# Gated delta net: a new order of steps over the engines' queues, and the decayed state made by four VectorE operations per chunk

## The chip, the cores and the metric

The kernel runs on one core of a Trainium2 chip. The metric is the time of one execution on the device in microseconds (us); of several runs the median. A core has a matrix engine (TensorE, PE in the profile; PEld is its loading of weights), a vector engine (VectorE, DVE), an engine for activations and copies (ScalarE, ACT), a general one (GpSimd, POOL), and SyncE (SP), which issues DMAs. Each engine works through a queue of its own in order and waits at semaphores.

## The reference, cut to what matters

The network is two blocks of attention and experts; x is 2 x 512 tokens of 256. Only the delta net of the second block is touched by the change. For each of 32 value heads (two to each of 16 key heads) it works through 8 chunks of 64 tokens, one after the other, since each needs the state that the one before left:

```python
def chunk_step(state, c):
    ...
    intra = jnp.where(mask_upper1, 0.0, qk * dm_c)
    v_prime = v_c - jnp.einsum('bhld,bhde->bhle', kcd_c, state)
    inter = jnp.einsum('bhld,bhde->bhle', q_c, state) * ge_c[..., None]
    out = inter + jnp.einsum('bhij,bhjd->bhid', intra, v_prime)
    new_state = state * gel_c[..., None] + jnp.einsum('bhld,bhle->bhde', k_c * kd_c, v_prime)
    return (new_state, out)
```

Ahead of it, q, k, v and z are projected from x, q, k and v go through a causal convolution of four taps and silu, q and k are normed by the root of their sums of squares, and a triangular 64 x 64 matrix per chunk is inverted. Behind it, the output is multiplied by silu(z), normed, and projected by W_out.

## The kernel before, in words

Stages run one after the other: experts, attention, experts, experts (gelu), delta net, experts (gelu). The delta net (`delta_net`) goes over 16 key heads, each with its two value heads (GRP = 2) and both sequences (B = 2), so a state is a tile of 128 x (2 x 2 x 128) floats.

The order of all work is written out by hand as one list of steps, `whole_order`, which every engine walks through; each engine takes from a step its own part. While head j runs its chunks (the recurrence), the same list prepares head j + 1 (projections PR, taps TP, silu SL, sums of squares NM, coefficients, gram and decay GD, the inversion BS, gather, unit, mirror), begins head j + 2, and finishes head j - 1 (scale_out SC, turn_out TO, project_out PO). `head_order` has 24 slots for this; `pair_order` puts six of them among the steps of each pair of chunks: read_state, z, slot, new_values, e, slot, update, turn, slot, z, read_state, slot, new_values, e, slot, update, turn, slot. Slots are counted from 0 in the text. What a step does:

- proj (PR, number 0 to 11): TensorE projects 128 x 512 into bank A or C, and ScalarE copies it to raw (0 to 7) or through silu to zt (8 to 11). Bank A is also used by turn, bank C by gram.
- tap (TP): VectorE, one of four taps of the convolution over 128 x 1024, from raw to cv.
- norms (NM): TensorE sums the squares of q and k over partitions, with matmuls of one column against a vector of ones, into bank B. norm_roots: ScalarE's square root. coefs: VectorE copies and makes the coefficients of the head (cf). shares: GpSimd multiplies nbs by a coefficient.
- out_squares, out_norm: sum of squares of the output, root and reciprocal; scale_out: VectorE multiplies o by it; turn_out: TensorE turns it, ScalarE copies to oT; project_out: TensorE multiplies by wout, VectorE adds to x.
- read_state: TensorE multiplies k and q with state; VectorE makes wv (L1858), ScalarE makes qs. new_values: TensorE, then ScalarE copies vp. update: TensorE adds up k times vp into banks 0 and 1 (`added_to_state`), then VectorE makes the new state and o, and GpSimd multiplies o by zt (L1724).
- kept (GpSimd, L1718, in read_state): state times the decay of the chunk, for chunks 1 to 6. VectorE's update then adds kept and the banks (L1870).
- spread and gather: SyncE moves blocks through DRAM for the inversion; unit and mirror (VectorE) finish it, and z of the next head waits for both (G_r, mirror_r).
- rows: VectorE subtracts and caps the exponents x0, ScalarE takes exp, GpSimd masks (nbs).

Of the kernel before, what the change touches and what calls it, by code (L numbers as in the profile page):

```python
# [14 lines left out]
P = 128  # L15
# [1111 lines left out]
def steps_of(j):  # L1127

    exists = 0 <= j < HK
    several = lambda name: lambda *ns: [(name, j, n) for n in ns] if exists else []  # L1130
    PR = lambda *ns: [("proj", j, n, "AC"[n % 2]) for n in ns] if exists else []
    TP = lambda u, *ns: [("tap", j, u, n) for n in ns] if exists else []
    GD = lambda *cs: [(name, j, c) for c in cs for name in ("gram", "decay")] if exists else []
    PO = lambda n, *halves: [("project_out", j, n, q) for q in halves] if exists else []
    ONE = lambda *names: [(name, j) for name in names] if exists else []
    return PR, TP, GD, PO, ONE, several


def prepare_order(j):

    PR, TP, GD, _, ONE, several = steps_of(j)
    SL, NM, BS = several("silu"), several("norms"), several("base")
    yield from ONE("rows")
    for u in range(4):
        yield from PR(2 * u, 2 * u + 1) + TP(u, *range(CONV))
    yield from SL("k0", "k1", "q") + NM(0, 1, 2, 3) + ONE("norm_roots", "coefs", "shares") + GD(*range(0, NCH, 2))
    yield from ONE("spread") + SL("v0", "v1") + PR(8, 9, 10, 11) + BS(0, 1, 2, 3) + ONE("gather", "unit", "mirror")

# [32 lines left out]
def head_order(j):  # L1181

    PR, TP, GD, _, ONE, several = steps_of(j + 1)
    SL, NM, BS = several("silu"), several("norms"), several("base")
    PR2, TP2, _, _, ONE2, several2 = steps_of(j + 2)
    SL2 = several2("silu")
    _, _, _, PO, OUT, several0 = steps_of(j - 1)
# [12 lines left out]
    yield from pair_order((j, 2), (j, 4), (j, 6), slots[6:12])  # L1200
    yield from pair_order((j, 4), (j, 6), here(j + 1, 0), slots[12:18])
    yield from pair_order((j, 6), here(j + 1, 0), here(j + 1, 2), slots[18:24])


def whole_order():

    PR, TP, _, _, ONE, several = steps_of(1)
    SL = several("silu")
    yield from prepare_order(0)
    yield from [("turn", 0, 0), ("turn", 0, 1)]  # L1210
    yield from pair_order(None, (0, 0), (0, 2), [
        PR(0) + ONE("rows"), PR(1), PR(2) + TP(0, 0), PR(3) + TP(0, 1, 2), TP(0, 3) + TP(1, 0) + SL("k0"), TP(1, 1, 2) + SL("k1")])
    for j in range(HK):
        yield from head_order(j)
    _, _, _, PO, OUT, several = steps_of(HK - 1)
    SC, TO = several("scale_out"), several("turn_out")
    yield from OUT("out_squares", "out_norm")
    for n in range(NCH // 2):
        yield from SC(n) + TO(n) + PO(n, 0, 1)


def delta_net(nc, m, tag, W_qkvz, W_ba, conv_w, A_log, dt_bias, norm_w, W_out, table, compact, eye16_in):
# [8 lines left out]
    with ExitStack() as ctx:  # L1231
# [13 lines left out]
        raw = sb("raw", [P, 3, B, CONV - 1 + T])  # L1245
# [29 lines left out]
        kept = sb("kept", [P, B, GRP, DK])  # L1275
# [8 lines left out]
        pe_sems = "pj ss_r A_r C_r Z_r E_r PK_r PQ_r V_r SP_r I_r ot_r yp".split()  # L1284
        act_sems = "ev X_e sl srt A_e E_x WT_r qs_r vp_r sq_r srt2 oT_r".split()
        dve_sems = "cvd sm_r cf_r row_r X_r C_e base_c base_r mirror_r G_r Zi_r w_r S_r of_r ssq_r ms_r on_r y_done chain".split()
        pool_sems = "st_r z16 EN_r kept_r oz_r".split()
# [47 lines left out]
        def _(sp):  # L1335
# [22 lines left out]
            def step(i, name, j, *a):  # L1358
# [5 lines left out]
                elif name == "rows" and kh + 1 < HK:  # L1364
# [35 lines left out]
        def _(pe):  # L1400
# [3 lines left out]
            last_bank = [None]  # L1404

            def step(i, name, j, *a):
                kh = head(i, j)
                if name == "proj":
# [5 lines left out]
                    wait(pe, "ev", kh * 12 + (mth if where == last_bank[0] else mth - 1))  # L1414
                    last_bank[0] = where
# [17 lines left out]
                elif name == "norms":  # L1433

                    quarter, = a
                    if quarter == 0:
                        wait(pe, "sl", kh * 5 + 3)
                        wait(pe, "sm_r", kh)
                        wait(pe, "oT_r", so_far["turn_out"])
                        wait(pe, "y_done", so_far["project_out"])  # L1440
                    for n in range(quarter * 4, quarter * 4 + 4):
                        c, b = n // B, n % B
                        for u in range(2):
                            for h in range(GRP):
                                mm = pe.matmul(bB[h * C:(h + 1) * C, u * NBC + n:u * NBC + n + 1],
                                               sq[:, u, b, c * C:(c + 1) * C], ones[:], start=True, stop=True)
                    if quarter == 3:
                        mm.then_inc(s_["ss_r"], 1)
                elif name == "turn":
# [6 lines left out]
                    wait(pe, "ev", so_far["proj"])  # L1456
# [5 lines left out]
                elif name == "gram":  # L1462
# [5 lines left out]
                    wait(pe, "ev", so_far["proj"])  # L1468
# [110 lines left out]
        def _(act):  # L1579
            copy = lambda out, in_, **kw: nc.scalar.activation(out, in_, ACT.Copy, **kw)  # L1580

            def step(i, name, j, *a):
                kh, f = head(i, j), j % 2
                if name == "proj":
# [3 lines left out]
                    if mth in (0, 6):  # L1588
                        wait(act, "cvd", kh * 4 + mth // 6)
                    source = bA if a[1] == "A" else bC  # L1590
                    if u < 4:
                        copy(raw[:, u % 3, b, CONV - 1:], source).then_inc(s_["ev"], 1)
# [6 lines left out]
                elif name == "silu":  # L1599
# [6 lines left out]
                    by_chunk = lambda t: t.rearrange("p (c n) -> p c n", c=NCH)  # L1606
                    if what[0] == "k":
# [34 lines left out]
                elif name == "rows":  # L1642
# [58 lines left out]
        def _(pool):  # L1701
            def step(i, name, j, *a):
                kh, f = head(i, j), j % 2
                if name == "rows":
# [3 lines left out]
                elif name == "shares":  # L1708
# [3 lines left out]
                    nc.gpsimd.tensor_tensor(nbs[:], nbs[:], down_head(cf[f][:, C_NBETA2, :]), ALU.mult).then_inc(s_["EN_r"], 1)  # L1712
# [21 lines left out]
        def _(dve):  # L1734
# [19 lines left out]
            def step(i, name, j, *a):  # L1754
                kh, f = head(i, j), j % 2
                if name == "tap":
# [3 lines left out]
                    if tap == 0:  # L1760
# [4 lines left out]
                        ins = nc.vector.tensor_scalar(cv[:, u], raw[:, u % 3, :, 0:T], cw[:, g, 0:1], None, ALU.mult)  # L1765
                    else:
                        chained(i)
                        ins = nc.vector.scalar_tensor_tensor(out=cv[:, u], in0=raw[:, u % 3, :, tap:tap + T], scalar=cw[:, g, tap:tap + 1],  # L1768
# [5 lines left out]
                elif name == "norms" and a[0] == 3:  # L1774
                    wait(dve, "ss_r", kh + 1)

                    nc.vector.tensor_scalar(roots[:], bB[:, 0:NBC], 1e-6, None, ALU.add)
                    nc.vector.tensor_scalar(cf[f][:, C_QEPS, :], bB[:, NBC:2 * NBC], 1e-6, float(DK) * 1e-6, ALU.add,
                                            ALU.mult).then_inc(s_["sm_r"], 1)
                elif name == "coefs":  # L1780
# [3 lines left out]
                    wait(dve, "EN_r", kh - 1)  # L1784
# [6 lines left out]
                elif name == "rows":  # L1791
                    dve.wait_ge(row_loaded, kh * 32 + 32)
                    wait(dve, "E_x", kh)
                    nc.vector.tensor_tensor(x0[:], x0[:], down_head(coef[:, kh, K_CUM, :]), ALU.subtract).then_inc(s_["row_r"], 1)
                    wait(dve, "row_r", kh + 1)
                    nc.vector.scalar_tensor_tensor(out=x0[:], in0=x0[:], scalar=-CLIP, in1=over_head(cap),
                                                   op0=ALU.max, op1=ALU.min).then_inc(s_["X_r"], 1)
                elif name == "decay":
# [7 lines left out]
                    wait(dve, "EN_r", kh + 1)  # L1806
# [153 lines left out]
```

## Time and profile before

| | us |
|---|---|
| median of 3 runs | 2825.47 |
| lowest and highest | 2804.49, 2827.88 |
| profiled execution | 2823.2 |
| its span | 2821.5 |
| TensorE busy in it | 2484.1 (88%) |
| VectorE busy | 1655.0 (59%) |
| ScalarE busy | 1092.7 (39%) |
| GpSimd busy | 345.9 (12%) |

The profile is of one execution. "Busy" of an engine is the time in which it has an instruction at work; the ends of matmuls are modelled. "Idle before" is the time ahead of an instruction in which its engine did nothing, with the instruction whose end released it.

### The profile page before, as it was taken

To read this page: it belongs to the slowest core of one execution; us is meant where nothing else is said; L and a number is where in the kernel's file an instruction comes from. 1 tells how busy PE (TensorE), PEld (TensorE's weight loads), DVE (VectorE), ACT (ScalarE), POOL (GpSimd) and SP (SyncE) were. 2 spreads that over 40 slices of the span, in tenths; PEclk is the share of its full clock that TensorE was granted. 3 is DMA by queue.
4 is the path that set the end of the run, shared out by engine and by line. 5 is a ranking of instruction groups with operands and counts; after the bars stand their busy time and mean duration, and the time that the engine had idled before them with its cause. 6 is when DMAs were issued, how large, how long until landed. Compare 5 with 4: busy or idle time off the path is not lost. (4 is left out here: it accounts for less than half of the span.)

```text
span 2821.5 us, 57806 instructions
## 1 busy us (share of the span) xinstructions
PE 2484.1 (88%) x22866; PEld 1886.6 (67%) x22866; DVE 1655.0 (59%) x3456; ACT 1092.7 (39%) x2364; POOL 345.9 (12%) x348
## 2 busy tenths in 40 slices
PE   7899897999983688899889888898988888699998
PEld 4443455999971466676666676676766676599997
DVE  4434346575642466667656766667666754657563
ACT  1113313232211345555555545555545534223221
POOL 0001100000000012222121221222221212000000
PEclk9879898999995789999999999999999988699998
DMA  1100011101001100111001110111001100110100
GB/s 44 33 1 1 12 33 61 61 30 59 30 5 36 27 19 15 28 32 28 22 15 31 32 28 9 28 32 31 21 16 28 24 9 9 61 61 30 59 30 15
DMA packets 135592, 80.85 MB, mean 29 GB/s; under 512 B 86592, under 2 KB 125008, under 8 KB 135376
## 3 DMA queue, kind: packets, MB, share of 16 engines
q1 hardware_dynamic: 135376, 77.82, 10.0%
q8 instruction: 154, 2.52, 0.4%
q14 instruction: 62, 0.51, 0.1%
HBM read 72.41 MB, written 5.37 MB: 28 GB/s over the span
## 5 line engine op out<-in xcount | busy, mean ns | idle before, releaser
L1423 PE MATMUL dn_ps<-xnT,dn_w 128*128 128x512 f32 x512 | 270.2, 655 | 48.9 <-ACT dn_vt L1580 31.1
L435 ACT ACTIVATE g_h<-g_ps,g_b_now 128x512 f32<-128x512 f32 x256 | 175.0, 689 | 338.2 <-PE g_ps L459 332.4
L472 PE MATMUL g_ps<-g_w_low,g_h_high 128*128 128x256 f32 x1024 | 289.8, 283 | 0.0
L472 PE MATMUL g_ps<-g_w_high,g_h_low 128*128 128x256 f32 x1024 | 289.8, 283 | 0.0
L472 PE MATMUL g_ps<-g_w_high,g_h_high 128*128 128x256 f32 x1024 | 289.7, 283 | 0.0
L1768 DVE SCALAR_TENSOR_TENSOR dn_cv<-dn_raw,dn_cw,dn_cv 128x1024 f32<-128x1024 f32 x192 | 270.1, 1407 | 2.6
L459 PE MATMUL g_ps<-g_x_high,g_w_high 128*128 128x512 f32 x512 | 201.9, 394 | 18.0 <-DVE g_w_low L516 15.6
L459 PE MATMUL g_ps<-g_x_low,g_w_high 128*128 128x512 f32 x512 | 201.2, 393 | 0.0
L459 PE MATMUL g_ps<-g_x_high,g_w_low 128*128 128x512 f32 x512 | 200.7, 392 | 0.0
L472 PEld LDWEIGHTS g_ps<-g_w_high,g_h_high 128*128 128x128 f32 x1024 | 196.5, 192 | 0.9
L472 PEld LDWEIGHTS g_ps<-g_w_low,g_h_high 128*128 128x128 f32 x1024 | 196.5, 192 | 0.9
L472 PEld LDWEIGHTS g_ps<-g_w_high,g_h_low 128*128 128x128 f32 x1024 | 196.5, 192 | 0.0
L1423 PEld LDWEIGHTS dn_ps<-xnT,dn_w 128*128 128x128 f32 x512 | 95.7, 205 | 132.1 <-issue 119.2
L516 DVE TENSOR_TENSOR g_h_low<-g_h,g_h_high 128x512 fp32r<-128x512 f32 x256 | 177.3, 693 | 8.8
L565 DVE SCALAR_TENSOR_TENSOR x_res<-g_ps,g_w,x_res 128x256 f32<-128x256 f32 x128 | 61.7, 482 | 171.8 <-PE g_ps L472 171.8
L513 DVE CAST g_h_high<-g_h 128x512 fp32r<-128x512 f32 x256 | 109.0, 426 | 78.9 <-ACT g_h L435 77.8
L1565 PE MATMUL dn_ps<-dn_wout,dn_oT 128*128 128x256 f32 x512 | 148.2, 414 | 6.5 <-ACT dn_oT L1580 4.1
L1430 PE MATMUL dn_ps<-dn_w,xnT 128*64 128x128 f32 x2048 | 126.4, 277 | 19.9 <-ACT dn_vt L1580 19.9
L1580 ACT ACTIVATE dn_raw<-dn_ps 128x512 f32<-128x512 f32 x128 | 76.5, 598 | 151.1 <-PE dn_ps L1423 151.1
L1580 ACT ACTIVATE dn_qs<-dn_ps,dn_cf 128x128 f32<-128x128 f32 x224 | 70.2, 364 | 161.5 <-PE dn_ps L1515 161.4
L1430 PEld LDWEIGHTS dn_ps<-dn_w,xnT 128*64 128x64 f32 x2048 | 112.1, 138 | 27.8 <-issue 25.8
L1718 POOL TENSOR_TENSOR dn_kept<-dn_state,dn_cf 128x512 f32<-128x512 f32 x96 | 128.9, 1343 | 0.0
(273 smaller groups left out, 4977.8 us busy)
## 6 DMA issues: line engine op xcount, KB each, us to landing
g_w<-in_fc_dram SPq DMA_DIRECT2D x32, 1024.0 KB, 6.4
dn_w<-in_W_qkvz_dram SPq DMA_DIRECT2D x16, 768.0 KB, 4.3
dn_x<-dn_cum_rows SPq DMA_DIRECT2D x32, 256.0 KB, 3.9
dn_wout<-in_W_out_dram SPq DMA_DIRECT2D x16, 256.0 KB, 2.6
f_gate<-in_gateT_dram SPq DMA_DIRECT2D x16, 128.0 KB, 2.1
f_up<-in_upT_dram SPq DMA_DIRECT2D x16, 128.0 KB, 2.3
f_down<-in_downT_dram SPq DMA_DIRECT2D x16, 128.0 KB, 2.5
dn_blocks_rows<-dn_ge SPq DMA_DIRECT2D x128, 16.0 KB, 1.7
```

Of the source, the lines that this page charges most:

```text
L435: nc.scalar.activation(h[:, f % 4], h_b[f % 4], ACT.Gelu, bias=b1_now[u // 2][:, f:f + 1]).then_inc(h_ready, 1)
L459: last = pe.matmul(h_b[f % 4], weights[:, k, f * P:(f + 1) * P], x[:, k, half * BANK:(half + 1) * BANK], start=(k == 0 and n == 0), stop=( ...
L472: last = pe.matmul(y_b[q % 2][:, 0:D], hidden[:, f, q * P:(q + 1) * P], weights[:, f, :], start=(f == 0 and n == 0), stop=(f == NF - 1 and ...
L513: nc.vector.tensor_copy(high, whole).then_inc(high_made, 1)
L516: return nc.vector.tensor_tensor(low, whole, high.bitcast(F32), ALU.subtract)
L565: nc.vector.scalar_tensor_tensor(out=m.x[:, t, :], in0=y_b[q % 2][:, 0:D], scalar=w[:, bass.ds(2 * i + u // 2, 1), t], in1=m.x[:, t, :], o ...
L1423: mm = pe.matmul(to, w[:, k, W_COL[u] * P:(W_COL[u] + 1) * P], m.xnT[:, k, b * T:(b + 1) * T], start=(k == 0), stop=(k == KD - 1))
L1430: mm = pe.matmul(to[half(h), part(n)], m.xnT[:, k, b * T + c * C:b * T + (c + 1) * C], w[:, k, W_COL[4 + h] * P:(W_COL[4 + h] + 1) * P], s ...
L1565: mm = pe.matmul(projected, tokens, wout[:, h, :], start=(h == 0), stop=(h == GRP - 1))
L1580: copy = lambda out, in_, **kw: nc.scalar.activation(out, in_, ACT.Copy, **kw)
L1718: nc.gpsimd.tensor_tensor(kept[:], state[:], last_decay.broadcast_to([P, B, GRP, DK]), ALU.mult).then_inc(s_["kept_r"], 1)
L1768: ins = nc.vector.scalar_tensor_tensor(out=cv[:, u], in0=raw[:, u % 3, :, tap:tap + T], scalar=cw[:, g, tap:tap + 1], in1=cv[:, u], op0=AL ...
```

## The change

- The slots of `head_order` and `whole_order` are filled in another order, and each projection now names its bank (A or C). A projection waits for the copy of the last projection in the same bank, no longer for that of the last one at all; so do turn and gram. raw has four buffers, not three.
- The sums of squares are made by operand (k, then q) and sequence, in four steps of their own, k's as soon as its squares are there; k's and q's results have semaphores of their own (sm_r, qm_r).
- rows is split in rows and caps, out_norm in out_norm and out_recip; shares is done in two halves with a semaphore each.
- kept is gone. VectorE makes the new state in four operations, one for each sequence and value head: state times the decay plus the banks.

```diff
     slots = [
-        PR(4) + TP(1, 3) + OUT("out_squares"), PR(5) + SL("q"), NM(0, 1) + TP(2, 0), NM(2, 3) + TP(2, 1),
-        PR(6) + ONE("norm_roots") + OUT("out_norm") + TP(2, 2), PR(7) + ONE("coefs", "shares") + SC(0) + TP(2, 3),
-        TO(0) + SL("v0") + GD(0), PO(0, 0) + GD(2), PO(0, 1) + GD(4) + SC(1), TO(1) + GD(6) + ONE("spread") + TP(3, 0),
-        PO(1, 0) + TP(3, 1), PR(8) + TP(3, 2),
-        PR(9) + TP(3, 3) + BS(0), PR(10) + BS(1) + SL("v1") + SC(2), PR(11) + BS(2), PO(1, 1) + BS(3) + ONE("gather", "unit"),
-        TO(2) + PR2(0) + ONE2("rows"), PO(2, 0) + PR2(1),
-        PO(2, 1) + ONE("mirror") + TP2(0, 0), PR2(2) + TP2(0, 1), PR2(3) + TP2(0, 2) + SC(3), TO(3) + TP2(0, 3) + TP2(1, 0),
-        PO(3, 0) + TP2(1, 1) + SL2("k0"), PO(3, 1) + TP2(1, 2) + SL2("k1")]
+        PR(4, "A") + TP(1, 3) + OUT("out_squares") + SL("k0", "k1"), PR(5, "C") + NM(0, 0), PR(6, "C") + NM(0, 1) + SL("q") + TP(2, 0),
+        PR(7, "A") + NM(1, 0) + ONE("norm_roots") + OUT("out_norm") + TP(2, 1),
+        PR(8, "C") + NM(1, 1) + ONE("coefs", "shares") + OUT("out_recip") + TP(2, 2) + SC(0), TO(0) + GD(0),
+        PR(9, "A") + GD(2) + TP(2, 3), PO(0, 0) + GD(4) + TP(3, 0), PO(0, 1) + GD(6) + ONE("spread") + SL("v0") + SC(1),
+        PR(10, "A") + TO(1) + TP(3, 1), PR(11, "C") + TP(3, 2), PO(1, 0) + BS(0),
+        PR2(0, "A") + TP(3, 3) + BS(1), PR2(1, "C") + SL("v1") + BS(2), PR2(2, "C") + BS(3) + ONE("gather") + ONE2("rows"),
+        PR2(3, "A") + TP2(0, 0), PO(1, 1) + TP2(0, 1) + SC(2), TO(2) + ONE("unit", "mirror"),
+        PO(2, 0) + TP2(0, 2), PO(2, 1) + TP2(0, 3), ONE2("caps") + SC(3),
+        TO(3) + TP2(1, 0), PO(3, 0) + TP2(1, 1), PO(3, 1) + TP2(1, 2)]
...
-                    wait(pe, "ev", kh * 12 + (mth if where == last_bank[0] else mth - 1))
-                    last_bank[0] = where
+                    wait(pe, "ev", last_proj[where])
+                    last_proj[where] = kh * 12 + mth + 1
...
-                elif name == "read_state":
-                    c, = a
-                    if 0 < c < NCH - 1:
-                        wait(pool, "S_r", stateful(i, j, c))
-                        last_decay = cf[f][:, K_GL:K_GL + GRP, B * c:B * c + B].rearrange("p h b -> p b h")[:, :, :, None]
-                        nc.gpsimd.tensor_tensor(kept[:], state[:], last_decay.broadcast_to([P, B, GRP, DK]), ALU.mult).then_inc(s_["kept_r"], 1)
+                    for n in range(2):
+                        rows = slice(n * NBC // 2, (n + 1) * NBC // 2)
+                        shares = cf[f][:, C_NBETA2, rows][:, :, None].broadcast_to([P, NBC // 2, C])
+                        nc.gpsimd.tensor_tensor(nbs[:, rows], nbs[:, rows], shares, ALU.mult).then_inc(s_["EN_r"], 1)
...
-                elif name == "norms" and a[0] == 3:
+                elif name == "norms" and a == (0, B - 1):
                     wait(dve, "ss_r", kh + 1)
 
-                    nc.vector.tensor_scalar(roots[:], bB[:, 0:NBC], 1e-6, None, ALU.add)
+                    nc.vector.tensor_scalar(roots[:], bB[:, 0:NBC], 1e-6, None, ALU.add).then_inc(s_["sm_r"], 1)
+                elif name == "norms" and a == (1, B - 1):
+                    wait(dve, "sq_sum", kh + 1)
                     nc.vector.tensor_scalar(cf[f][:, C_QEPS, :], bB[:, NBC:2 * NBC], 1e-6, float(DK) * 1e-6, ALU.add,
-                                            ALU.mult).then_inc(s_["sm_r"], 1)
+                                            ALU.mult).then_inc(s_["qm_r"], 1)
...
-                            wait(dve, "kept_r", i * 12 + (6 * j + c))
-                            nc.vector.tensor_tensor(state[:], kept[:], added_to_state, ALU.add).then_inc(s_["S_r"], 1)
+                            for b in range(B):
+                                for h in range(GRP):
+                                    last = nc.vector.scalar_tensor_tensor(out=state[:, b, h, :], in0=state[:, b, h, :],
+                                                                          scalar=col(cf[f], K_GL + h, c, b), in1=added_to_state[:, b, h, :],
+                                                                          op0=ALU.mult, op1=ALU.add)
+                            last.then_inc(s_["S_r"], 1)
```

## Rows read from the trace of the kernel before

**Rows 1.** The page, busy time of each engine: us, share, instructions.

```profile
PE 2484.1 (88%) x22866; PEld 1886.6 (67%) x22866; DVE 1655.0 (59%) x3456; ACT 1092.7 (39%) x2364; POOL 345.9 (12%) x348
```

**Rows 2.** Windows: the delta net's stage, then one head of it.

```profile
core 0: us, PE busy (x) PEld busy (x) DVE busy (x) ACT busy (x) POOL busy (x), PEclk, DMA share, GB/s
895.00:2440.00 1545.00, 1328.21 (x16304) 997.07 (x16304) 964.66 (x2084) 775.58 (x1886) 313.03 (x259) 0.92 0.10 25
...
1537.40:1626.30 88.90, 79.96 (x1002) 60.59 (x1000) 59.37 (x128) 48.12 (x117) 19.75 (x16) 0.95 0.11 25
```

**Rows 3.** Waits of TensorE over 13 heads: us, times, longest us.

```profile
PE dn_ps L1528 <- DVE dn_wv L1858: 22.7, 13, 1.8
PE dn_ps L1423 <- ACT dn_vt L1580: 22.1, 13, 1.7
PE dn_ps L1430 <- ACT dn_vt L1580: 17.2, 13, 1.3
PE dn_ps L1497 <- DVE dn_w L1843: 15.3, 13, 1.2
PE dn_ps L1511 <- DVE dn_state L1870: 13.4, 13, 1.1
PE dn_ps L1445 <- ACT dn_cv L1620: 10.9, 12, 0.9
```

**Rows 4.** Windows around the falls of the granted clock, first and last of 13.

```profile
1177.00:1181.00 4.00, 4.00 (x68) 3.87 (x68) 1.19 (x4) 0.34 (x2) 0.00 (x0) 0.57 0.00 0
...
2256.00:2270.00 14.00, 14.00 (x170) 11.24 (x168) 2.64 (x7) 1.93 (x8) 0.45 (x1) 0.51 0.01 3
```

**Rows 5.** Timeline of TensorE: sums of squares without a fall, then with one.

```profile
1088.45 2.03 PE L1445 MATMUL dn_ps<-dn_ones,dn_cv 128*64 128x1 f32 x64 [0.91 <-ACT dn_cv L1620]
...
1534.39 2.38 PE L1445 MATMUL dn_ps<-dn_ones,dn_cv 128*64 128x1 f32 x64 [0.91 <-ACT dn_cv L1620]
...
1539.51 3.52 PE L1445 MATMUL dn_ps<-dn_ones,dn_cv 128*64 128x1 f32 x64
```

**Rows 6.** The tile kept: duration in ns, minimum, median, maximum.

```profile
L1718 POOL TENSOR_TENSOR dn_kept<-dn_state,dn_cf x96: 1036/1049/2032, 1006.1 to 2369.7; 128x512 f32<-128x512 f32 x96
L1870 DVE TENSOR_TENSOR dn_state<-dn_kept,dn_ps x96: 675/681/690, 1021.3 to 2373.7; 128x512 f32<-128x512 f32 x96
```

**Rows 7.** Timeline of VectorE: start us, us, line, operation.

```profile
1552.24 0.22 DVE L1785 COPY dn_cf<-dn_coef 128x128 f32<-128x128 f32 x1
...
1553.49 0.69 DVE L1892 TENSOR_TENSOR dn_o<-dn_o,dn_rms 128x512 f32<-128x512 f32 x1
1554.09 2.92 DVE L1768 SCALAR_TENSOR_TENSOR dn_cv<-dn_raw,dn_cw,dn_cv 128x1024 f32<-128x1024 f32 x1
1556.94 0.60 DVE L1858 SCALAR_TENSOR_TENSOR dn_wv<-dn_ps,dn_cf,dn_vt 128x128 f32<-128x128 f32 x2
...
1570.30 1.28 DVE L1768 SCALAR_TENSOR_TENSOR dn_cv<-dn_raw,dn_cw,dn_cv 128x1024 f32<-128x1024 f32 x1
...
1590.39 1.21 DVE L1838 TENSOR_TENSOR dn_ge<-dn_ge,dn_eye 128x1024 f32<-128x1024 f32 x1
```

**Rows 8.** Timeline of GpSimd in the same stretch.

```profile
1553.66 2.28 POOL L1712 TENSOR_TENSOR dn_nbs<-dn_nbs,dn_cf 128x1024 f32<-128x1024 f32 x1 [0.53 <-DVE dn_cf L1790]
1555.90 2.02 POOL L1718 TENSOR_TENSOR dn_kept<-dn_state,dn_cf 128x512 f32<-128x512 f32 x1
```

**Rows 9.** Timeline of TensorE: projections 11 and 0, then an update and a turn.

```profile
1584.06 1.97 PE L1430 MATMUL dn_ps<-dn_w,xnT 128*64 128x128 f32 x32
...
1590.40 1.98 PE L1423 MATMUL dn_ps<-xnT,dn_w 128*128 128x512 f32 x4
1592.31 0.71 PE L1540 MATMUL dn_ps<-dn_vp,dn_kdk 64*128 64x128 f32 x8
1592.96 0.65 PE L1544 MATMUL dn_ps<-dn_vp,dn_intra 64*64 64x128 f32 x8
1593.54 0.44 PE L1458 MATMUL dn_ps<-ident,dn_qkk 128*128 128x128 f32 x2
1593.82 0.38 PE L1460 MATMUL dn_ps<-ident,dn_vv 128*128 128x128 f32 x2
1594.04 1.03 PE L1565 MATMUL dn_ps<-dn_wout,dn_oT 128*128 128x256 f32 x4
```

**Rows 10.** Timeline of ScalarE: silu and square of k.

```profile
1612.32 1.28 ACT L1610 ACT_TABLE_LOAD   x1
1613.62 1.06 ACT L1610 ACTIVATE dn_qkk<-dn_cv 128x1024 f32<-128x1024 f32 x1
1614.70 0.63 ACT L1613 ACTIVATE dn_cv<-dn_qkk 128x512 f32<-128x512 f32 x1
```

**Rows 11.** Timeline of TensorE in the last head.

```profile
2344.84 0.66 PE L1511 MATMUL dn_ps<-dn_state,dn_qkk 128*64 128x128 f32 x8 [0.99 <-DVE dn_state L1870]
```

More of the change, by code:

```diff
@@ L1130, in steps_of @@
     several = lambda name: lambda *ns: [(name, j, n) for n in ns] if exists else []
-    PR = lambda *ns: [("proj", j, n, "AC"[n % 2]) for n in ns] if exists else []
+    PR = lambda n, bank: [("proj", j, n, bank)] if exists else []
     TP = lambda u, *ns: [("tap", j, u, n) for n in ns] if exists else []
     GD = lambda *cs: [(name, j, c) for c in cs for name in ("gram", "decay")] if exists else []
+    NM = lambda u, *bs: [("norms", j, u, b) for b in bs] if exists else []
     PO = lambda n, *halves: [("project_out", j, n, q) for q in halves] if exists else []
     ONE = lambda *names: [(name, j) for name in names] if exists else []
-    return PR, TP, GD, PO, ONE, several
+    return PR, TP, GD, PO, NM, ONE, several
 def prepare_order(j):
-    PR, TP, GD, _, ONE, several = steps_of(j)
-    SL, NM, BS = several("silu"), several("norms"), several("base")
-    yield from ONE("rows")
+    PR, TP, GD, _, NM, ONE, several = steps_of(j)
+    SL, BS = several("silu"), several("base")
+    yield from ONE("rows", "caps")
     for u in range(4):
-        yield from PR(2 * u, 2 * u + 1) + TP(u, *range(CONV))
-    yield from SL("k0", "k1", "q") + NM(0, 1, 2, 3) + ONE("norm_roots", "coefs", "shares") + GD(*range(0, NCH, 2))
-    yield from ONE("spread") + SL("v0", "v1") + PR(8, 9, 10, 11) + BS(0, 1, 2, 3) + ONE("gather", "unit", "mirror")
+        yield from PR(2 * u, "A") + PR(2 * u + 1, "C") + TP(u, *range(CONV))
+    yield from SL("k0", "k1", "q") + NM(0, 0, 1) + NM(1, 0, 1) + ONE("norm_roots", "coefs", "shares") + GD(*range(0, NCH, 2))
+    yield from ONE("spread") + SL("v0", "v1") + PR(8, "A") + PR(9, "C") + PR(10, "A") + PR(11, "C")
+    yield from BS(0, 1, 2, 3) + ONE("gather", "unit", "mirror")
 def pair_order(done, build, front, slots=[[]] * 6):
@@ L1205, in whole_order @@
 def whole_order():
-    PR, TP, _, _, ONE, several = steps_of(1)
-    SL = several("silu")
+    PR, TP, _, _, _, ONE, _ = steps_of(1)
     yield from prepare_order(0)
@@ L1244, in delta_net @@
         nw = sb("nw", [P, 1])
-        raw = sb("raw", [P, 3, B, CONV - 1 + T])
+        raw = sb("raw", [P, 4, B, CONV - 1 + T])
         cv = sb("cv", [P, 4, B, T])
@@ L1363, in step @@
                     load_taps(kh + 1)
-                elif name == "rows" and kh + 1 < HK:
+                elif name == "caps" and kh + 1 < HK:
                     load_rows(kh + 1)
@@ L1433, in step @@
                 elif name == "norms":
-                    quarter, = a
-                    if quarter == 0:
+                    u, b = a
+                    if u == 0:
+                        wait(pe, "sl", kh * 5 + b + 1)
+                    else:
                         wait(pe, "sl", kh * 5 + 3)
-                        wait(pe, "sm_r", kh)
+                        wait(pe, "sm_r", kh + 1)
+                    if u == b == 0:
+                        wait(pe, "qm_r", kh)
                         wait(pe, "oT_r", so_far["turn_out"])
                         wait(pe, "y_done", so_far["project_out"])
[L1441 to L1448, printed above, removed]
+                    for c in range(NCH):
+                        n = c * B + b
+                        for h in range(GRP):
+                            mm = pe.matmul(bB[h * C:(h + 1) * C, u * NBC + n:u * NBC + n + 1],
+                                           sq[:, u, b, c * C:(c + 1) * C], ones[:], start=True, stop=True)
+                    if b == B - 1:
+                        mm.then_inc(s_["sq_sum" if u else "ss_r"], 1)
                 elif name == "turn":
@@ L1587, in step @@
                     wait(act, "pj", kh * 12 + (mth + 1))
-                    if mth in (0, 6):
-                        wait(act, "cvd", kh * 4 + mth // 6)
+                    if u < 4:
+                        wait(act, "cvd", kh * 4 - 4 + (u + 1))
                     source = bA if a[1] == "A" else bC
                     if u < 4:
-                        copy(raw[:, u % 3, b, CONV - 1:], source).then_inc(s_["ev"], 1)
+                        copy(raw[:, u, b, CONV - 1:], source).then_inc(s_["ev"], 1)
                     else:
@@ L1606, in step @@
                     by_chunk = lambda t: t.rearrange("p (c n) -> p c n", c=NCH)
+                    if what == "q":
+                        wait(act, "sq_sum", kh)
                     if what[0] == "k":
@@ L1641, in step @@
                     last.then_inc(s_["A_e"], 1)
-                elif name == "rows":
+                elif name == "caps":
                     wait(act, "X_r", kh + 1)
@@ L1703, in step @@
                 kh, f = head(i, j), j % 2
-                if name == "rows":
+                if name == "caps":
                     wait(pool, "E_x", kh + 1)
```

45 lines of the change are left out of this document (22 added, 23 removed).

## The prediction

> **What bounds the kernel now.** I read in this order: the page's busy times, the stages as windows, the waits of TensorE, and one head of the delta net as a timeline. TensorE is busy 88% of the span, VectorE 59% [rows 1]; the delta net, the only stage that the diff touches, takes 1545 us, some 89 us per head [rows 2]. In the head shown TensorE works 79.96 of 88.9 us. It is in order, so its time is its work plus the idle gaps ahead of steps whose input is late. Over 13 heads the same gaps come back once each [rows 3]: 1.75 us for dn_wv, 1.7 and 1.3 for a projection whose bank waits for the turned copies (dn_vt), 1.2 for the mirror (dn_w), 1.1 for the state, 0.9 for the squares of q (dn_cv), and about 1 for the rest: 8.9 us a head. The second loss is the clock. In 13 of the 14 times from 1088 us on that the sums of squares are made, the granted clock falls from 2.4 to 1.2 GHz, in stretches of 4 to 15 us that begin at the sums; ahead of the fall TensorE had idled 0.9 us and run one-column matmuls, 64 in a row [rows 4, 5]. Once, at 1088 us, it doesn't fall behind the same 0.9 us of idleness [rows 5]. At 1.2 GHz the 64 take 3.5 us, at 2.4 GHz 2.0 [rows 5]; such differences, added over the ten low microseconds of the head shown, give some 4.5 us lost, 0.45 for each, and with a mean of 8.2 low microseconds a head (each window's width times twice what its clock lacks to 1, over 14) 3.7. So the head shown is 75.5 us of work at full clock, 8.9 of gaps, 4.5 of clock. What can be won is in the last two.
>
> **The state on VectorE.** Before, GpSimd makes kept in 1.05 us, up to 2.03, right after the previous state, with time to spare: nobody waits for it. VectorE then adds in 0.68 us [rows 6]. This became four operations of 128x128 with one operand in the banks. The nearest row is L1858, the same kind and size: two of them take 0.60 us, so 0.27 each behind the first, and four take about 1.15 (bounds: 0.68, one operation of the same size in all [rows 6], and 1.4 for four durations of 0.35, a pair of 0.60 less the second's 0.27, laid end to end). The step is 0.6 us in the queue today, so each of 96 chunks costs VectorE 0.5 us more (0.1 to 0.8): 3 us a head, 4% of a queue with 29 us free. It lies on the path only where TensorE arrives before the state; I count that within the stalls below. What is won: kept no longer collides. A GpSimd operation of 1.05 us took 2.02 beside a tap [rows 8].
>
> **The places.** I walked the new order of slots along the three queues with durations of the trace: projection 1.91 us, update 1.23 and turn 0.50 by the distances of starts [rows 9], a tap 1.2, unit, mirror and caps 1.15 to 1.2 each, wv 0.6 [rows 7], silu 1.06 and square 0.63 with a table load of 1.28 ahead [rows 10]. Work is the same; the gaps move.
> - Gone: both dn_vt gaps (3.0 us). Projections into bank A now stand in the first or fourth slot of a pair, never right behind a turn. Gone too the 0.9 at the squares of q and the 1.1 and 1.75 where the state and dn_wv stood behind the reciprocal and the long tap. The taps cost nothing more, with a fourth raw buffer, and the weight DMA keeps its 4.4 us between the end of projection 11 (1586.0) and the next projection 0 (1590.4) [rows 9], by my walk 4.4 again.
> - Slots 0 and 1: SL(k0, k1) now stands on ScalarE between the copy of projection 4 and vp. From the end of projection 4: copy 0.5, squares 0.6, load 1.3, silu and square of k0 1.7, so the sums for k0 start at +4.2 where TensorE is ready at +3.3 (0.8 idle); k1 another 1.7 and vp 0.6, so the update starts at +6.3 against +5.4 (0.9 idle). 1.7 in all.
> - Slots 4 and 5, the largest: C_QEPS waits for the last sums, and VectorE has coefs, the reciprocal, tap (2, 2) and SC(0) queued behind it, while TensorE has only the update and a turn, 1.7 us, before TO(0) waits for SC(0). coefs take 1.25 (1552.24 to 1553.49), the reciprocal 0.3, tap 1.2, scaling 0.6, ends and semaphores 0.4: 3.7, so at least 2.0 idle. At the same moment GpSimd starts the two halves of nbs, 1.15 each. Today that tap took 2.92 instead of 1.28 us: it waited until nbs was done [rows 7, 8]. If the tap waits for one half, 3.1 idle; if SC(0) also waits for the other, 4.2. I take 3.1, as GpSimd's operation gave way to the waiting tap between nbs and kept.
> - Slot 13: the turn of the next head waits for SL(v1), 0.5, as today.
> - Slots 16 to 18: from the end of PO(1, 1) VectorE has add 0.4, tap 1.2, SC(2) 0.6, state 1.15, o 0.3, sum 0.6, unit 1.15, mirror 1.15, wv 0.6; TensorE has update, turn, TO(2), read, z, PO(2, 0), 5.0 us. It idles 0.6 for SC(2), 0.6 for the state, 1.0 for unit (z needs G_r) and 0.2 for wv: 2.4.
> - Slots 19 to 21: the tap, the state, caps 1.2 and SC(3) stand before wv; slot 20 has nothing for TensorE. Idle 0.4 (state), 1.1 (SC(3)), 0.4 (wv): 1.9.
>
> Gaps after: 1.7 + 3.1 + 0.5 + 2.4 + 1.9 = 9.6 us against 8.9: +0.7 a head, with bounds of -0.4 (2.0 at slot 5) and +1.8 (4.2).
>
> **The port rule.** The tap stood still while nbs ran [rows 7, 8]. The Trainium skill, page "SBUF — State Buffer", section "Who interferes with whom", says that a VectorE instruction with two SBUF inputs and a GpSimd one that reads SBUF exclude each other for the whole instruction, while one with a single SBUF input isn't touched. The trace agrees in the one row. By the rule the new state operations (one input in the banks) never collide, and SC(0), with two inputs in SBUF, can: it makes the 4.2 of the bound possible and rules no term out.
>
> **The clock after the change.** No row shows the sums split in four. Bounds: the fall never comes (-3.7 us a head) or comes as today and once more at the gap of slot 5, which is longer than any gap of today's heads (+1.5, the shortest of today's falls, 3.4 us, at 0.45). For the first speaks that a projection of full columns now stands right ahead of each quarter of the sums; for the second that in slot 1 idle, sums and idle follow each other for 2.9 us, much like the 0.9 and 2.4 ahead of today's fall, and the 3 us at slot 5. The stretch in slot 1 is the nearest to today's, and I take a fall of four fifths of today's length: -0.8.
>
> **The last head** has no projections to hide latency: its gap before reading the state is 0.99 us [rows 11]. Four operations add 0.5 there in up to six chunks: +2 (0 to 3). The first head gains and loses nothing that I can find.
>
> **The sum.** 15 heads x (0.7 - 0.8) + 2 = 0 us, on the profiled execution's own 2823.2 us (its span of 2821.5 and 1.7 around it). The median of the three runs is 2.3 us above that execution, so 2826. The lowest of them is 0.7% below the median, so 1% (28 us, 1.9 us a head) is about what this measurement tells from no change.
>
> **Rivals.**
> - The clock holds. The sums are spread enough, and at slot 5 only 2.0 us are idle: (-0.4 - 3.7) x 15 + 2 = -59: 2766. For it: no gap of today outside the sums, up to 1.75 us long, comes with a fall, and at 1088 us the sums didn't bring one either [rows 3 to 5]. Against: the gap behind the last sums.
> - VectorE's chain behind the last sums takes the clock too. Place: C_QEPS to SC(0), slot 4. Price 4.2 us of gap, and a second fall: (1.8 + 1.5) x 15 + 3 = +52: 2878. It decides once the tap and SC(0) both wait for GpSimd. For it: the 2.92 us tap. Against: half an nbs is half as long.
> - The change does less than it says: the state operations take their time inside today's gaps and the gaps stay by place. Then only the last head shows it: +2, 2828, inside the forecast's own range of 2800 to 2855.
>
> **How the numbers follow.** Forecast with the third rival 0.40, clock holds 0.31, chain and clock 0.29. The walk has small latencies left out and could be off by 1 us a head beside that; the range reaches to the rivals' times: 2764 to 2882. Faster by over 1% (under 2797) 0.31, within 1% 0.39, slower 0.30.
>
> **What would show it.** In the profile after: the lines for dn_vt as a releaser of projections gone (right) or still near 17 us (wrong). TensorE idle 2 to 4.2 us once a head ahead of TO(0) (L1555), until the scaling of o, and some 1 us each until unit, the state or SC(3) near TO(2) and TO(3). Four state operations in 1.1 to 1.2 us, none stretched. nbs in two parts with a stretched tap beside the first. The granted clock in the sums: 2.4 GHz all the way makes the first rival true. The forecast fails if TO(0) finds SC(0) done, which would mean that I walked slot 4 wrongly, or if the clock's loss vanishes or doubles.

## The result, and the profile after

The changed kernel takes 2829.3 us (median of 20 runs) where the kernel before takes 2816.5 (20 runs): ratio 1.0044, with an interval of 1.0026 to 1.0062. It is slower by 13 us, under the 1% that I had called telling. The profiled execution (2841.7 us, span 2840.0) lies 12 us above its own median, and that of before 7 us above; so the difference of the two traces, 18.5 us, overstates the loss, and single terms are compared below within traces.

TensorE does the same 22866 matmuls [rows 1]. The page of after, busy times:

```profile
PE 2500.2 (88%) x22866; PEld 1888.8 (67%) x22866; DVE 1690.5 (60%) x3744; ACT 1087.9 (38%) x2364; POOL 236.0 (8%) x268
```

It is busy 16.1 us longer than before for the same matmuls, and idle (span less busy) 339.8 us where it was 337.4. So 16 of the 18.5 us between the two traces are slower matmuls, and 2.4 are idleness. The granted clock of the whole execution is 0.917 where it was 0.923, which makes some 36 more microseconds at the low clock.

What holds TensorE from 1092.9 to 2249 us, the stretch that [rows 3] covers, waits of after (us in all, times, longest us):

```profile
PE dn_ps L1558 <- DVE xn L1901: 32.5, 19, 3.2
PE dn_ps L1558 <- DVE dn_o L1901: 29.5, 18, 3.4
PE dn_ps L1488 <- DVE dn_ge L1843: 13.5, 12, 1.1
PE dn_ps L1543 <- ACT dn_vp L1583: 12.3, 12, 1.0
PE dn_ps L1448 <- ACT dn_cv L1618: 9.7, 12, 0.8
PE dn_ps L1423 <- DMA dn_w<-in_W_qkvz_dram: 9.6, 12, 1.7
PE dn_ps L1514 <- DVE dn_state L1876: 7.6, 24, 0.3
PE dn_ps L1461 <- ACT dn_vv L1629: 5.2, 13, 0.4
PE dn_ps L1531 <- DVE dn_wv L1863: 2.3, 12, 0.2
```

Both lines of dn_vt, dn_wv's 1.75 us and the mirror are gone, as walked. In their place, half of all idleness stands ahead of turn_out (L1558), which waits for VectorE's scaling of o (its tiles are xn and dn_o); then come unit (L1843), vp, the squares of k and the weights' DMA. One such gap, timeline of TensorE:

```profile
1557.11 0.38 PE L1463 MATMUL dn_ps<-ident,dn_vv 128*128 128x128 f32 x2
1560.71 1.09 PE L1558 MATMUL dn_ps<-ident,dn_o 128*128 128x128 f32 x4 [3.23 <-DVE dn_o L1901]
1561.59 1.92 PE L1473 MATMUL dn_ps<-dn_qkk 128*128 128x128 f32 x8
```

VectorE in the same microseconds: C_QEPS when the last sums are there, coefs, then the tap and SC(0), and the four state operations:

```profile
1555.72 0.17 DVE L1782 TENSOR_SCALAR dn_cf<-dn_ps 128x16 f32<-128x16 f32 x1 [5.40 <-PE dn_ps L1448]
...
1557.18 1.94 DVE L1770 SCALAR_TENSOR_TENSOR dn_cv<-dn_raw,dn_cw,dn_cv 128x1024 f32<-128x1024 f32 x1
1559.04 1.52 DVE L1901 TENSOR_TENSOR dn_o<-dn_o,dn_rms 128x512 f32<-128x512 f32 x1
1560.49 1.11 DVE L1876 SCALAR_TENSOR_TENSOR dn_state<-dn_state,dn_cf,dn_ps 128x128 f32<-128x128 f32 x4
```

And GpSimd, with both halves of nbs merged in one row:

```profile
1557.00 3.02 POOL L1720 TENSOR_TENSOR dn_nbs<-dn_nbs,dn_cf 128x512 f32<-128x512 f32 x2 [13.84 <-DVE dn_cf L1794]
```

VectorE sat idle for 5.40 us waiting for the sums, and then did 4.8 us of work that TO(0) was waiting for. Tap and scaling took 1.94 and 1.52 us instead of 1.28 and 0.68 next to nbs. The gap is 3.23 us. Taken singly, the first half of nbs took 1.04 us and the second, behind the tap's start, 2.02: the two engines held each other up in turn.

The granted clock fell from 2.4 to 1.2 GHz twice in most heads, once near the first sums and once at this gap; the eight gram matmuls behind it take 1.92 us, at full clock 1.05. Windows around both falls of a head, the first and the last of twelve (columns as in [rows 2], the granted clock third from the end):

```profile
1169.00:1196.00 27.00, 23.56 (x302) 18.36 (x304) 11.97 (x30) 13.09 (x31) 4.47 (x4) 0.81 0.00 1
...
2183.00:2213.00 30.00, 25.75 (x332) 19.98 (x332) 12.08 (x30) 14.78 (x34) 4.47 (x4) 0.77 0.01 2
```

At 0.81 over 27 us that is 10.3 low microseconds, at 0.77 over 30 us 13.8; the twelve windows give a mean of 12.9, against 8.2 before [rows 4]. Over the same 1156 us, the windows row of before and of after:

```profile
1092.90:2249.00 1156.10, 1034.34 (x13022) 779.63 (x13020) 767.72 (x1655) 618.82 (x1506) 254.50 (x206) 0.96 0.10 25
```

```profile
1092.90:2249.00 1156.10, 1033.85 (x12688) 769.47 (x12686) 774.00 (x1843) 593.77 (x1459) 158.34 (x138) 0.93 0.10 25
```

TensorE was busy equally long in both, and in after it did 334 matmuls fewer in that time, at a clock of 0.93 for 0.96.

Where in the stage the time went is seen from the first state of each head, timeline of VectorE: heads 1, 2, 15 and 16 of before, then of after:

```profile
L1867 DVE COPY dn_state<-dn_ps x16: 691/692/693, 1003.9 to 2337.6; 128x512 f32<-128x512 f32 x16
...
1086.42 0.69 DVE L1867 COPY dn_state<-dn_ps 128x512 f32<-128x512 f32 x1 [2.04 <-PE dn_ps L1540]
...
2253.17 0.69 DVE L1867 COPY dn_state<-dn_ps 128x512 f32<-128x512 f32 x1 [2.04 <-PE dn_ps L1540]
```

```profile
L1872 DVE COPY dn_state<-dn_ps x16: 690/692/693, 1000.5 to 2356.6; 128x512 f32<-128x512 f32 x16
...
1078.03 0.69 DVE L1872 COPY dn_state<-dn_ps 128x512 f32<-128x512 f32 x1 [5.04 <-PE dn_ps L1543]
...
2278.42 0.69 DVE L1872 COPY dn_state<-dn_ps 128x512 f32<-128x512 f32 x1 [4.87 <-PE dn_ps L1543]
```

The 13 full heads between take 92.3 us each instead of 89.8: +34 us. The way to the first state is 3.4 us shorter, the first head 5.1 and the next to last 6.2. These ends give back 15 us. Most of that is the clock as well. Windows of the first head and of the next to last, before, then after:

```profile
1003.86:1086.42 82.56, 73.24 (x970) 55.21 (x972) 52.62 (x115) 44.65 (x109) 19.34 (x16) 0.92 0.10 24
2253.17:2337.56 84.39, 74.36 (x994) 60.35 (x996) 48.25 (x119) 38.04 (x104) 16.84 (x15) 0.88 0.06 11
```

```profile
1000.54:1078.03 77.49, 67.37 (x970) 50.54 (x972) 53.66 (x133) 44.56 (x109) 14.06 (x11) 1.00 0.11 26
2278.42:2356.64 78.22, 68.11 (x962) 55.51 (x964) 49.37 (x136) 37.84 (x105) 9.22 (x10) 0.93 0.06 12
```

In the first head TensorE does the same 970 matmuls in 67.4 us instead of 73.2, at a clock of 1.00 for 0.92, and its idleness grows by 0.8 us. In the next to last, with 32 matmuls fewer, its idleness is the same 10 us, and the clock is 0.93 for 0.88. Before had a fall in the first head and two in the next to last; after has none and two shorter ones. Only the 3.4 us ahead of the first state are idleness saved.

### The profile page after: what moved, and what is told of

It reads as the page before. It is cut to its first block and busy times, and to the rows that moved or that the text cites. A ratio compares the mean times of both kernels' runs of the same rounds, so it can differ in the third digit from the quotient of the medians.

```text
span 2840.0 us, 58055 instructions
## 1 busy us (share of the span) xinstructions
PE 2500.2 (88%) x22866; PEld 1888.8 (67%) x22866; DVE 1690.5 (60%) x3744; ACT 1087.9 (38%) x2364; POOL 236.0 (8%) x268
## 5 line engine op out<-in xcount | busy, mean ns | idle before, releaser
L1770 DVE SCALAR_TENSOR_TENSOR dn_cv<-dn_raw,dn_cw,dn_cv 128x1024 f32<-128x1024 f32 x192 | 257.0, 1338 | 2.7
L459 PE MATMUL g_ps<-g_x_high,g_w_high 128*128 128x512 f32 x512 | 202.1, 395 | 17.5 <-DVE g_w_low L516 15.6
L1583 ACT ACTIVATE dn_kdk<-dn_ps,dn_cf 128x128 f32<-128x128 f32 x256 | 79.9, 363 | 222.1 <-PE dn_ps L1463 222.1
L1876 DVE SCALAR_TENSOR_TENSOR dn_state<-dn_state,dn_cf,dn_ps 128x128 f32<-128x128 f32 x384 | 107.2, 341 | 51.8 <-PE dn_ps L1543 51.7
L459 PEld LDWEIGHTS g_ps<-g_x_high,g_w_high 128*128 128x128 f32 x512 | 97.4, 190 | 38.1 <-issue 15.8
```

Source lines behind the costliest of these rows:

```text
L459: last = pe.matmul(h_b[f % 4], weights[:, k, f * P:(f + 1) * P], x[:, k, half * BANK:(half + 1) * BANK], start=(k == 0 and n == 0), stop=( ...
L1876: last = nc.vector.scalar_tensor_tensor(out=state[:, b, h, :], in0=state[:, b, h, :], scalar=col(cf[f], K_GL + h, c, b), in1=added_to_stat ...
```

## The experiments

All ratios are to the kernel before, timed on the same chip.

**The state operations alone: state_only.** The kernel before, in its own order:

```diff
-                            wait(dve, "kept_r", i * 12 + (6 * j + c))
-                            nc.vector.tensor_tensor(state[:], kept[:], added_to_state, ALU.add).then_inc(s_["S_r"], 1)
+                            for b in range(B):
+                                for h in range(GRP):
+                                    last = nc.vector.scalar_tensor_tensor(out=state[:, b, h, :], in0=state[:, b, h, :],
...
```

The lines of kept on GpSimd go too.

> The kernel before, in its own order, with kept taken away and the four operations of VectorE per chunk in its place. Theory W (the time is the gaps of TensorE and its clock; the places moved them): each state is made 0.5 us later where VectorE is late already, which is once a head (the read ahead of TO(0) and what follows), so +0.5 us a head, +8 us, about +0.3% on before (0.1% to 0.6%). Rival S (the four operations are what costs): 3 us a head of VectorE's queue come out as time, +45 us, +1.6%.

Measured: 1.0043 (1.0012 to 1.0073), 12 us. In its trace one wait of TensorE has grown, that for the state, from 13.4 us [rows 3] to

```profile
PE dn_ps L1511 <- DVE dn_state L1865: 18.9, 13, 1.5
```

and all others stand as before: 0.4 us a head in the one place where VectorE is late. W's size, not S's. Over the whole execution that wait grows by 7.0 us (15.6 to 22.6), of 12 in all; the rest is within the interval.

**The places alone: places_only.** The changed kernel with kept and the one addition back.

> The changed kernel with kept back on GpSimd and one addition on VectorE per chunk; all places as in the changed one. W: the two gaps of 0.3 us ahead of reading the state close and the chain to unit and wv is 0.5 us shorter, against some collisions of kept with taps: 0.5 to 1.3 us a head less than the changed kernel, -8 to -20 us, so within 0.3% of before either way. The 3.2 us gap ahead of TO(0) and both falls of the clock stay. S: the whole difference to before and more goes, 1% or more faster than before.

Measured: 1.0010 (0.9988 to 1.0031), 2823 us. The moved places by themselves made no difference that this measures. The four operations cost 0.4% in the order of before; in the new order it is the 0.34% between this run and the changed kernel, whose intervals overlap a little. That is at the low edge of what W expected. S falls.

**GpSimd out of the way: shares_late.**

```diff
                     wait(pool, "st_r", kh + 1)
+                    wait(pool, "on_r", kh * 4 - 7)
                     for n in range(2):
```

> The changed kernel with one wait more: GpSimd's two halves of nbs wait until SC(0) is done, so they can't stand in the way of tap (2, 2) and SC(0). W: the tap takes 1.28 and SC(0) 0.69 us instead of 1.94 and 1.52, the gap ahead of TO(0) shrinks from 3.2 to 1.9 us, nobody waits for nbs: -1.3 us a head, -19 us on the changed kernel if the clock falls as before, about -35 if that fall goes, so -0.2% to -0.8% on before. Rival (the gap has another cause, VectorE's own order): the gap stays above 2.5 us.

Measured: 0.9847 (0.9818 to 0.9876), 2776 us, 54 less than the changed kernel and better than the range expected. Waits, the gap ahead of TO(0) in one head, and window of its trace:

```profile
PE dn_ps L1558 <- DVE xn L1902: 23.6, 21, 1.7
PE dn_ps L1558 <- DVE dn_o L1902: 22.2, 19, 1.9
```

```profile
1527.26 0.63 PE L1558 MATMUL dn_ps<-ident,dn_o 128*128 128x128 f32 x4 [1.72 <-DVE dn_o L1902]
```

```profile
1092.90:2249.00 1156.10, 1046.81 (x13612) 785.14 (x13612) 802.32 (x1958) 635.28 (x1560) 156.30 (x148) 0.99 0.11 25
```

The gap is 1.72 us in 13 of 14 heads (1.9 the longest), where it was 3.23: a little less than the 1.9 expected, and worth some 21 us over 14 heads. The rest, some 33, goes with the clock, 0.99 instead of 0.93. I had expected 35 us in all where the fall goes; falls near the first sums became rare as well, and why they did is not shown.

**The gap filled with useless work: fill_gap.** Two matmuls more ahead of TO(0)'s wait:

```diff
+                    if n == 0 and kh < HK - 2:
+                        for k in range(KD):
+                            pe.matmul(bB, m.ident[:], m.xnT[:, k, 0:T], start=True, stop=True)
                     wait(pe, "on_r", kh * 4 + (n + 1))
```

> The changed kernel with two matmuls of 128x512 more in each head, of no use, put into the gap ahead of TO(0): 1.9 us of work in 3.2 us of idleness, into a bank that the turn writes over; nothing that the kernel waits for ends sooner. W with the clock as a term of its own: the gap's end stays where it is, but the granted clock no longer falls there, 6.7 low microseconds a head at 0.45, up to -42 us on the changed kernel (ratio to before 0.990 to 1.000). Rival (the fall is owed to the sums of squares ahead, or the loss of clock lies beside other waits and costs nothing): the time stays at +0.4% on before or grows.

Measured: 0.9911 (0.9885 to 0.9938), 2792 us, 37 less than the changed kernel, though it does more. Timeline of TensorE and window:

```profile
1534.69 1.88 PE L1558 MATMUL dn_ps<-xnT,ident 128*128 128x512 f32 x4
1537.99 0.66 PE L1561 MATMUL dn_ps<-ident,dn_o 128*128 128x128 f32 x4 [1.42 <-DVE dn_o L1904]
1538.49 1.06 PE L1473 MATMUL dn_ps<-dn_qkk 128*128 128x128 f32 x8
```

```profile
1092.90:2249.00 1156.10, 1049.62 (x13310) 772.29 (x13310) 804.94 (x1911) 622.79 (x1525) 167.18 (x145) 0.98 0.10 25
```

TO(0) still waits for the scaling, and starts 3.3 us after the turn (1.88 of useless matmuls, 1.42 of idleness) where it was 3.23. Nothing that it waits for came sooner. Only the clock held there: gram takes 1.06 us, and no fall at this gap is left in the 13 full heads. Near the first sums one of 3.4 us stays in most heads. This shows the clock as a cost of its own, and its size. The Trainium skill, page "TensorE: Matmul & The Clock Gate", section "What's actually happening", has the clock follow how busy the engine has recently been; these rows agree.

**The same in the kernel before: fill_before.** One matmul of 128x512 in the 0.9 us ahead of the sums, its wait for "sl" moved behind it.

> The kernel before, its order untouched, with one matmul of 128x512 more in each head, of no use, in the 0.9 us in which TensorE waits for the squares of q ahead of the sums. It takes 0.95 us, so the sums start up to 0.3 us later. W: the fall of the clock at the sums becomes rarer or shorter (8.2 low microseconds a head before, at 0.45: up to -3.7 us a head, -52 us; half of that if the 64 one-column matmuls behind it bring a fall by themselves half of the time): ratio 0.982 to 1.000. Rival (the sums alone lower the clock): 1.001 to 1.003, from the added matmul.

Measured: 0.9881 (0.9847 to 0.9915), 2786 us. The clock of the stretch is 0.99:

```profile
1092.90:2249.00 1156.10, 1041.28 (x13539) 779.55 (x13540) 791.85 (x1708) 635.43 (x1553) 266.13 (x215) 0.99 0.11 25
```

Of the 14 times from 1081 us on that the sums are made, four still come with a fall, two of these only behind the sums; in before it was 13 of 14. So in most heads the sums don't lower the clock by themselves: it took the idleness ahead of them too. The useless matmul brings 31 us, more than the whole change moved.

**VectorE's order in slot 4: sc_first.** The tap and SC(0) go where VectorE idled 5.40 us:

```diff
-        PR(8, "C") + NM(1, 1) + ONE("coefs", "shares") + OUT("out_recip") + TP(2, 2) + SC(0), TO(0) + GD(0),
+        PR(8, "C") + TP(2, 2) + OUT("out_recip") + SC(0) + NM(1, 1) + ONE("coefs", "shares"), TO(0) + GD(0),
```

> The changed kernel with slot 4 in another order: tap (2, 2), the reciprocal of the output's norm and SC(0) stand ahead of the last sums of squares and the coefficients, in the 5.4 us in which VectorE waits for these sums. W: no gap ahead of TO(0) (3.2 us a head less, -45 us), and if the idleness there is what lowers the clock the second time, that fall goes too (6.7 low microseconds at 0.45, -3 us a head, another -40): 2740 to 2785 us where before is 2816, ratio 0.973 to 0.989. Rival (the clock falls for the sums alone, whatever the gap): the gap goes, the second fall stays, ratio 0.988 or more.

Measured: 0.974 (0.9714 to 0.9766), 2746 us, 84 less than the changed kernel and within the range expected. What is left ahead of turn_out is SC(2) and SC(3) near the end of the head:

```profile
PE dn_ps L1558 <- DVE xn L1901: 11.6, 14, 1.1
...
PE dn_ps L1558 <- DVE dn_o L1901: 9.9, 12, 1.1
```

**Silu of k ahead of projections 4 and 5: k0_first.**

```diff
-        PR(4, "A") + TP(1, 3) + OUT("out_squares") + SL("k0", "k1"), PR(5, "C") + NM(0, 0), PR(6, "C") + NM(0, 1) + SL("q") + TP(2, 0),
+        SL("k0") + PR(4, "A") + TP(1, 3) + OUT("out_squares"), SL("k1") + PR(5, "C") + NM(0, 0), PR(6, "C") + NM(0, 1) + SL("q") + TP(2, 0),
```

> The changed kernel with silu and squares of k moved on ScalarE: those of sequence 0 ahead of projection 4, those of sequence 1 into slot 1. W: the gaps of 0.8 (ahead of the first sums) and 1.0 us (ahead of the first update) go, -1.8 us a head, -26 us, and with them the first fall of the clock, 3.4 to 6.8 low microseconds a head at 0.45, -20 to -40 more: 0.983 to 0.992 of before. The gap ahead of TO(0) and the second fall stay. Rival (ScalarE is late anyway, the gap moves to the copies of projection 4 or 5): within 0.5% of the changed kernel.

Measured: 0.9829 (0.9803 to 0.9855), 2773 us, at the good end of the range expected. Both waits for ScalarE (vp, dn_cv) are gone from its list, and TO(0)'s gap and fall have stayed:

```profile
1443.64 1.09 PE L1558 MATMUL dn_ps<-ident,xn 128*128 128x128 f32 x4 [3.23 <-DVE xn L1901]
```

**Both: sc_k0.**

> Both moves together: slot 4 reordered as in the run sc_first, and silu of k as in k0_first. W: sc_first's 2746 us less 1.8 us a head and less most of its remaining falls: 2700 to 2725, ratio 0.959 to 0.967, and hardly a fall of the clock left in the loop over heads. Rival: the two gains overlap, no better than 0.970.

Measured: 0.956 (0.9535 to 0.9586), 2695 us, a little better than expected. In the 13 full heads, which here end at 2138 us, the clock doesn't fall; in the stretch it falls once, behind them. The stretch, and this fall:

```profile
1092.90:2249.00 1156.10, 1082.13 (x14384) 817.94 (x14380) 843.03 (x2072) 664.29 (x1658) 161.90 (x156) 1.00 0.11 26
...
2186.00:2189.00 3.00, 2.00 (x25) 1.89 (x25) 0.94 (x5) 0.84 (x3) 0.00 (x0) 0.50 0.18 49
```

**And the later slots: sc_k0_tail.**

```diff
-        PR2(3, "A") + TP2(0, 0), PO(1, 1) + TP2(0, 1) + SC(2), TO(2) + ONE("unit", "mirror"),
-        PO(2, 0) + TP2(0, 2), PO(2, 1) + TP2(0, 3), ONE2("caps") + SC(3),
+        PR2(3, "A") + TP2(0, 0) + ONE("unit"), TP2(0, 1) + SC(2) + PO(1, 1), TO(2) + ONE("mirror"),
+        PO(2, 0) + TP2(0, 2), PO(2, 1) + TP2(0, 3), SC(3) + ONE2("caps"),
```

> As sc_k0, with the later slots in another order for VectorE too: unit in slot 15 and tap (0, 1) and SC(2) ahead of the wait for project_out (1, 1) in slot 16, where VectorE idles 3 us; SC(3) ahead of caps in slot 20. W: the gaps until SC(2), the state, unit and SC(3) shrink from 3.6 to about 0.6 us a head, -42 us on sc_k0: 2660 to 2690 us, ratio 0.945 to 0.955. Rival (the state's four operations, 1.1 us, hold the later slots by themselves): less than half of that gain.

Measured: 0.947 (0.9445 to 0.9495), 2668 us: the best version, 149 us under before. The gain on sc_k0 is 27 us, not 42: unit and SC(2) no longer stand in the way, but dn_wv now does, 19.2 us over some 14 heads (2.5 in sc_k0). The clock also falls again in four of the 13 full heads, for 3.4 us each; at 0.45 a low microsecond that is some 6 us.

```profile
PE dn_ps L1531 <- DVE dn_wv L1863: 19.2, 15, 1.3
```

**Its state back on GpSimd: best_kept.**

> As sc_k0_tail, but kept is back on GpSimd and VectorE adds it in one operation. W, with the gaps of TensorE mostly closed: the state comes 0.5 us sooner and the waits until dn_wv (19.2 us over 12 heads) shrink, but kept of 1.05 us blocks taps and scalings with two operands in SBUF, up to 1 us each: -0.5 to +0.5 us a head, ratio 0.944 to 0.950, no clear difference. Rival S (VectorE's 3 us a head more count once TensorE's gaps are gone): 15 to 45 us less, ratio 0.931 to 0.942.

Measured: 0.9528 (0.9494 to 0.9562), 2688 us. Neither: once the gaps are closed, kept on GpSimd is the slower way, by 20 us. One part shows in caps of VectorE (16 of them, us in all, mean ns), in best_kept, then in sc_k0_tail:

```profile
L1808 DVE SCALAR_TENSOR_TENSOR dn_x<-dn_x,dn_cap 128x1024 f32<-128x1024 f32 x16 | 26.5, 1654 | 0.0
```

```profile
L1801 DVE SCALAR_TENSOR_TENSOR dn_x<-dn_x,dn_cap 128x1024 f32<-128x1024 f32 x16 | 19.5, 1217 | 0.0
```

Caps reads two operands in SBUF. In 13 of 16 heads it takes 1.75 us instead of 1.22, but what runs beside it is not kept. It is GpSimd's product of o and zt, which in this order starts 0.43 us ahead of caps. Timeline of both engines in one head of best_kept:

```profile
1540.87 1.10 POOL L1733 TENSOR_TENSOR xn<-xn,dn_zt 128x256 f32<-128x256 f32 x1 [5.92 <-DVE xn L1889]
1541.30 1.75 DVE L1808 SCALAR_TENSOR_TENSOR dn_x<-dn_x,dn_cap 128x1024 f32<-128x1024 f32 x1
```

In places_only, with kept too, caps took 1.21 us. The wait for dn_wv grew from 19.2 to 24.8 us. Between the two profiled executions, 16 us apart, TensorE is idle 10 us more and busy 6 more; beyond the wait for dn_wv, what makes up the difference stays open.

## Why the prediction was right, and where not

I forecast 2826 us, "within 1%" as the likeliest case, and 2829 was measured. That the two lie 3 us apart is in part luck. The forecast was no change, on a first median of 2825.5; with 20 runs that median is 2816.5, and the change is +13 us. And wrong terms offset each other: by the sum the gaps were to bring +10 us, the clock -12, the last head +2. In the traces, where after is 18.5 us longer, gaps bring +2.4 and the clock +16.

- **The walk of the gaps held.** Against the trace, predicted and measured in us: slots 0 and 1, 0.8 and 0.9 against 0.81 and 1.0; TO(0) 3.1 against 3.23; SL(v1) 0.5, 0.4; SC(2) 0.6, 0.6; state 0.6 and 0.4, 0.3 twice; unit 1.0, 1.1; SC(3) 1.1, 1.1; dn_wv 0.6 in all, 0.2. In all 9.6 predicted and 9.8 measured a head (122.2 us of idleness in 12.5 heads), where before had 9.4 (I had counted 8.9). One term was missing: the next head's weights. I walked 4.4 us for their DMA, and TensorE waited up to 1.7, 0.8 on average.
- **TO(0)'s size was right for half the reason.** I let the tap wait for one half of nbs and SC(0) for none. Both were stretched, by 0.66 and 0.84 us, 1.5 together as against my 1.15. shares_late shows the collision to be worth the same 1.5 us of gap (3.23 less 1.72), and the rest, 1.7, to be VectorE's order, walked as 2.0. The exclusion that the Trainium skill states (page "SBUF — State Buffer", section "Who interferes with whom") was at work in both.
- **The state operations** took 1.11 us for my 1.15, none over 0.35 each beside GpSimd. Their cost, 0.4% by state_only and about 0.3% by places_only, shows in state_only as 7 us more of waiting for the state, not as the 3 us a head that VectorE's queue grew by.
- **The clock failed**: "I take a fall of four fifths of today's length: -0.8". It is the term mis-sized. Low microseconds a head went from 8.2 to 12.9 in the profiled execution; at my 0.45 that is +2.1, where the bound was +1.5. Both places that I had named for a fall had one. The price of 0.45 held: the same matmuls took 16.1 us more for some 36 more low microseconds, 0.45 each. fill_gap's profiled execution is 52 us below that of after, at a clock of the whole execution of 0.939 for 0.917, some 131 low microseconds fewer: 0.40 each.
- **The ends failed too**: I had +2 us for the last head and nothing for the first. They gave 15 us back. Gaps +0.4 and clock +2.1 make 2.5 a head, measured 2.6; 13 heads make +34, less 15 is the +19 between the spans. Some 11 of the 15 are the clock of the first and the next to last head, so the ends are in the main the clock term again, with the other sign. Why the clock falls there less is not shown.
- **The rivals.** The slower one, "VectorE's chain behind the last sums takes the clock too", named the right mechanism: a 3.2 us gap from C_QEPS to SC(0), and a second fall. Its size was not: 2.6 us a full head for its 3.3, since the gap was 3.2 and not 4.2, and the ends gave 15 back. The faster one, the clock holding, came true in all full heads only in sc_k0, where neither the scaling nor the first sums were waited for. The third rival's 2800 to 2855 is not the range that I gave in the end, 2764 to 2882.

## What to carry to other kernels

Look at the clock where TensorE idles next to instructions of few columns: here a gap of 3.2 us came with a fall of 6.8 us, some 3.1 us lost beside its own length, and one of 0.9 us with 8.2 low microseconds, 3.7 us lost. When steps move between slots, ask for each engine what its queue holds between the wait and the thing that another engine needs; putting independent work (a tap, a scaling) ahead of a wait instead of behind it was worth six times the whole change. Where two edits come together, run each alone: here the places gained nothing and the operations cost 0.4%, while an order a few lines away gained 4 to 5%.

## What the runs showed of the hardware that I had not expected

- Useless matmuls made two kernels faster, by 37 us (0.9911 against 1.0044) and by 31 us (0.9881 against 1), with the granted clock of the stretch up from 0.93 to 0.98 and from 0.96 to 0.99.
- Behind 0.9 us of idleness, 64 one-column matmuls came with a fall of the clock in 13 of 14 heads; with that idleness filled by one matmul of 128x512, in 4 of 14.
- In one head of the same 970 matmuls TensorE was busy 73.2 us at a granted clock of 0.92 and 67.4 at 1.00.
- A 128x128 SCALAR_TENSOR_TENSOR with one operand in the banks took 0.34 us and 0.26 behind another, and none of 384 was stretched (0.333 to 0.349), while a tap and a scaling with both in SBUF were stretched by 0.66 and 0.84 us beside the two halves of nbs, and the second half, 1.04 us when alone, by 0.98.
